# Moving shift rows from queries-on-partitions to rows: four TensorE transposes and a ScalarE copy, or one VectorE block transpose and four GpSimd copies

## What is computed

```
q, k, v = proj(xn, Wq, bq), proj(xn, Wk, bk), proj(xn, Wv, bv)      # (2, 16, 2048, 16)
idx = clip(r[None, :] - r[:, None], -128, 128) + 128
content = einsum('bhqd,bhkd->bhqk', q, k)
relative = einsum('bhqd,qkd->bhqk', q, rel_k[idx])
w = softmax((content + relative) / sqrt(16))
out = einsum('bhqk,bhkd->bhqd', w, v) + einsum('bhqk,qkd->bhqd', w, rel_v[idx])
s = out @ Wo.T + bo
h = gelu(einsum('td,edh->eth', xn, W1)); y = einsum('eth,ehd->etd', h, W2)
x + s * silu(y of the expert with the largest xn @ Wg + bg)
```

## Time and profile before

| | us |
|---|---|
| median of 3 runs | 2638.44 (2637.92 to 2640.88) |
| the profiled execution | 2641.73 |
| its span, first to last instruction | 2640.0 |
| PE busy | 2420.9 (92% of the span) |
| DVE busy | 1828.1 (69%) |
| ACT busy | 1749.4 (66%) |
| POOL busy | 884.5 (34%) |

### The profile page before, as it was taken

One profiled execution on the slowest core, in us unless ns is written; L12 is line 12 of the kernel. 1 busy time (PEld: TensorE's weight loads), 2 busy tenths in 40 slices (PEclk: granted clock), 3 DMA queues, 4 the chain that ended last, 5 costly groups with the idle time before them and its releaser, 6 DMA issues. The chain is left out here.

```text
span 2640.0 us, 47807 instructions
## 1 busy us (share of the span) xinstructions
PE 2420.9 (92%) x15216; PEld 1184.1 (45%) x15216; DVE 1828.1 (69%) x4985; ACT 1749.4 (66%) x4026; POOL 884.5 (34%) x1977
## 2 busy tenths in 40 slices
PE   6838999999999999999999999999999999799998
PEld 3412444444444444444444444444444444567666
DVE  6558777777777777777777777777777774233333
ACT  4514877777777777777777777777777777321121
POOL 1222454333333333333333333333333332133332
PEclk9955999999999999999999999999999999999999
DMA  5668889777777777777777777777777762642221
GB/s 160 176 141 265 244 268 243 235 222 230 233 230 237 225 222 233 234 231 236 232 228 234 231 236 236 231 226 226 233 231 238 227 194 88 244 144 69 66 64 53
DMA packets 351151, 541.00 MB, mean 205 GB/s; under 512 B 30608, under 2 KB 259392, under 8 KB 350912
## 3 DMA queue, kind: packets, MB, share of 16 engines
q1 hardware_dynamic: 336880, 502.76, 61.8%
q0 software_dynamic: 14032, 35.24, 4.5%
HBM read 272.60 MB, written 269.43 MB: 205 GB/s over the span
## 5 line engine op out<-in xcount | busy, mean ns | idle before, releaser
L1073 DVE TENSOR_REDUCE part<-ps 128x1 f32<-128x512 f32 (+3 forms) x2048 | 1189.5, 591 | 457.8 <-PE ps L957 438.8
L1135 ACT ACTIVATE probs_T<-pst 128x512 f32<-128x512 f32 (+3 forms) x2048 | 985.3, 525 | 397.4 <-PE pst L966 390.0
L957 PE MATMUL ps<-k_front,q_front 96*128 96x512 bf16 x2048 | 790.1, 393 | 13.0 <-DVE part L1071 2.5
L915 PE MATMUL pout<-probs_T,v_far 128*32 128x512 f32 (+3 forms) x4864 | 550.8, 533 | 40.4 <-ACT probs_T L1111 31.4
L822 POOL TENSOR_TENSOR left_T<-probs_T,left_mask 128x128 f32<-128x128 f32 x512 | 219.5, 429 | 991.7 <-ACT probs_T L1111 797.4
L957 PEld LDWEIGHTS ps<-k_front,q_front 96*128 96x128 bf16 x2048 | 198.6, 97 | 587.8 <-DVE part L1073 296.8
L966 PE MATMUL pst<-q_back,k_left 102*128 102x512 bf16 (+3 forms) x1024 | 349.7, 343 | 0.7 <-ACT probs_T L1135 0.6
L966 PE MATMUL pst<-q_back,k_right 102*128 102x512 bf16 (+3 forms) x1024 | 348.8, 342 | 0.5
L1148 ACT ACTIVATE band<-band,negm 128x384 f32<-128x384 f32 (+1 forms) x512 | 305.5, 597 | 0.1
L1071 DVE CUSTOM_DVE_ANT_0 band<-ps,band 128x256 f32<-128x256 f32 (+2 forms) x704 | 300.5, 427 | 0.0
L915 PEld LDWEIGHTS pout<-probs_T,v_far 128*32 128x32 f32 x4864 | 174.5, 108 | 237.9 <-issue 211.4
(11 more groups left out here) (160 smaller groups left out, 2112.0 us busy)
## 6 DMA issues: line engine op xcount, KB each, us to landing
rel_scores<-rel SPq DMA_DIRECT2D x128, 1024.0 KB, 7.9
band_probs<-band SPq DMA_DIRECT2D x128, 768.0 KB, 3.9
pwin<-band_probs SPq DMA_DIRECT2D x128, 512.0 KB
band<-rel_scores SPq DMA_DIRECT2D x64, 768.0 KB
band<-rel_scores SPq DMA_DIRECT2D x64, 576.0 KB, 5.2
w<-in_w_dram SPq DMA_DIRECT2D x16, 1024.0 KB, 14.3
band<-rel_scores SPq DMA_DIRECT2D x64, 128.0 KB, 5.7
q_terms<-terms SPq DMA_DIRECT2D x48, 128.0 KB
```

What stands on the lines that cost most here:

```text
L915: return nc.tensor.matmul(pout[32 * g:32 * g + 32, c0:c1], values, probs, start=first, stop=False, skip_group_check=True)
L957: nc.tensor.matmul(ps1[u % 2][:, :], q_front[a.par][:, a.s * P:(a.s + 1) * P], k_front[a.par][:, u * CW:(u + 1) * CW], start=True, stop=Tr ...
L1073: ins = nc.vector.tensor_reduce(peak, src, AX_X, ALU.max)
L1135: ins = nc.scalar.activation(probs_T[t.s % 2][:, u * CW + c0:u * CW + c1], pst[u % 2][:, c0:c1], ACT.Exp, scale=SCALE)
```

## The change

The shift values go into a `shb` of 32 columns for each block instead of 6 (zeroed once, so that the columns after the sixth are defined). In steps with off % 4 == 1, after the last maxima of the step, VectorE turns all 32x32 blocks of it into `shT` with one instruction of 128 partitions by 128 bf16. Query 32*b + c of block g then lies at partition 32*b + k, column (g, c), for shift row k. In steps with off % 4 == 2, at the very start of its step and so ahead of `left_T`, GpSimd copies the six rows of each of the four partition quarters into `q_back`, four instructions of 6 partitions by 4 x 32 bf16, each waiting for the one before. TensorE's four transposes, ScalarE's copy, and TensorE's waits that went with the shared bank are gone. Ahead of the copies GpSimd waits for VectorE's transpose, for earlier work of its own (`left_ready`, `sides_done`, `v_built`), and in hb 1 and 2 also for the `slot_tokens` DMAs of all steps before (`slots_filled`).

```diff
-        shb = two("shb", [P, CH, SHIFTS], BF16)
+        shb = two("shb", [P, CH, 32], BF16)
+        shT = sb("shT", [P, CH, 32], BF16)
-        prow = psmall[0:SHIFTS, NEARW:512].bitcast(BF16)
...
+                    pool.memset(shb[p][:, :, :], 0.0).then_inc(const_set, 1)
...
 # GpSimd, first thing in step(hb, off)
+                    q = Step(hb, off - 6)
+                    if off % CH == 2 and q.valid:
+                        pool.wait_ge(rows_tp, q.count(4, q.r + 1))
+                        if q.r == 0:
+                            wait(pool, st_mm, q.count(64, -64))
+
+                        left = Step(hb, off - LAG_T - 2)
+                        if left.valid:
+                            pool.wait_ge(left_ready, left.count(16, left.s + 1))
+                        sides = Step(hb, off + LAG_R - 4)
+                        pool.wait_ge(sides_done, sides.count(4, sides.r + 1) if sides.valid else NBH * 4)
+                        if off % NB == 10:
+                            pool.wait_ge(v_built, q.count(1, 1))
+                        if hb == 0:
+                            pool.wait_ge(slots_set, 16)
+                        if hb in (1, 2):
+                            pool.wait_ge(slots_filled, 16 * (TILES if hb == 2 else min(off, TILES)))
+                        rows = q_back[q.par][ROWS:ALLROWS, q.r * CW:(q.r + 1) * CW].rearrange("p (g b c) -> p b g c", g=CH, b=P // 32)
+                        for b in range(P // 32):
+                            if b > 0:
+                                pool.wait_ge(rows_link, q.count(12, 3 * q.r + b))
+                            ins = nc.gpsimd.tensor_copy(rows[:, b], shT[32 * b:32 * b + SHIFTS, :, :])
+                            ins.then_inc(rows_link if b < P // 32 - 1 else rows_copied, 1)
+                        pool.wait_ge(rows_copied, q.count(4, q.r + 1))
+
 # TensorE
-                    def shift_rows():
-
-                        pe.wait_ge(shift_ready, y.count(4, y.r + 1))
-                        wait(pe, rows_copied, y.count(4, y.r))
-                        if w.valid:
-                            wait(pe, winT_evac, w.count(16, w.s + 1))
-                        for g in range(CH):
-                            mm = nc.tensor.transpose(prow[0:SHIFTS, g * P:(g + 1) * P], shb[y.r % 2][:, g, :], con["ident_bf"][:, :])
-                        mm.then_inc(rows_tp, 1)
...
-                        if u == 1 and off % CH == 2 and y.valid:
-                            shift_rows()
...
-                        if off % CH == 2 and y.valid:
-                            pe.wait_ge(rows_copied, y.count(4, y.r + 1))
 # VectorE, after the maxima of u == 3
+                    def shift_rows():
+                        dve.wait_ge(shift_ready, shifted.count(4, shifted.r + 1))
+                        wait(dve, rows_copied, shifted.count(4, shifted.r))
+                        nc.vector.transpose(shT[:, :, :].rearrange("p g k -> p (g k)"), shb[shifted.r % 2][:, :, :].rearrange("p g k -> p (g k)")).then_inc(rows_tp, 1)
...
+                        if u == CH - 1 and off % CH == 1 and shifted.valid:
+                            shift_rows()
 # ScalarE
-                    def shift_rows():
-
-                        act.wait_ge(rows_tp, shifted.count(4, shifted.r + 1))
-                        nc.scalar.activation(q_back[shifted.par][ROWS:ALLROWS, shifted.r * CW:(shifted.r + 1) * CW], prow, ACT.Copy).then_inc(rows_copied, 1)
```

More of the change, by code:

```diff
@@ L605, in attend @@
         rows_tp = sem("rows_tp")
+        rows_link = sem("rows_link")
         rows_copied = sem("rows_copied")
@@ L683, in near_columns @@
             return bl[0] * P, (bl[-1] + 1) * P
-        CONSTS = 18
+        CONSTS = 20
         with nc.Block() as block:
@@ L828, in step @@
                         four = slice(4 * y.r, 4 * y.r + 4)
-                        t = shb[y.r % 2][:, :, :].rearrange("p g (k t) -> p g k t", k=2)
+                        t = shb[y.r % 2][:, :, 0:SHIFTS].rearrange("p g (k t) -> p g k t", k=2)
                         pool.wait_ge(rmax_ready, g + 1)
@@ L890, in step @@
                     w = Step(hb, off - LAG_T - 1)
-                    y = Step(hb, off - 6)
                     o = Step(hb, off - LAG_O)
                     ended = Step(hb, off - LAG_T - 2)
-                    def shift_rows():
-                        pe.wait_ge(shift_ready, y.count(4, y.r + 1))
-                        wait(pe, rows_copied, y.count(4, y.r))
-                        if w.valid:
-                            wait(pe, winT_evac, w.count(16, w.s + 1))
-                        for g in range(CH):
-                            mm = nc.tensor.transpose(prow[0:SHIFTS, g * P:(g + 1) * P], shb[y.r % 2][:, g, :], con["ident_bf"][:, :])
-                        mm.then_inc(rows_tp, 1)
                     def turn_back():
@@ L1023, in step @@
                     last = Step(hb, off - 1)
+                    shifted = Step(hb, off - 5)
                     four = slice(4 * last.r, 4 * last.r + 4)
@@ L1098, in step @@
                     y = Step(hb, off - 5)
-                    shifted = Step(hb, off - 6)
                     w = Step(hb, off - LAG_T - 1)
@@ L1140, in step @@
                             relative()
-                        if u == 1 and off % CH == 2 and shifted.valid:
-                            shift_rows()
                     if y.valid:
```

## The result

The change gains nothing: 2643.97 us (2639.76 to 2648.47, 10 runs) against 2638.49 (2633.72 to 2641.66, 10 runs), a ratio of 1.0021 with a 95% interval of 1.0011 to 1.0030. 2606 was predicted, with a range up to 2634. The span of the profiled execution is 2644.0 us against 2640.0.

The account below looks back on a forecast made before the run. PE's own work was taken to bound the kernel, with idle time before the transposes on its path. 2641.7 (profiled) - 66 (PE's gain) + 34 (second head's wait) = 2609.7, so a median of 2606 us; forecast 2592 to 2618, 8-in-10 range 2572 to 2634.

Parts of the forecast that it names:

- The bound and TensorE's gain: PE bounds the steps; without its transposes and their wait for VectorE's window it gains 65 to 67 us, taken as 66.
- ScalarE's copy, VectorE's transpose, GpSimd's copies: Removing 0.58 us copies gains nothing; a 0.25 us transpose and four 0.35 us copies a group cost nothing outside the second head.
- The room in steps 2 and 10: GpSimd's 1.75 us of copies a group fit without stopping PE: room 1.35 us in step 2, 1.1 in step 10.
- rival (c): Steps 2 and 10: GpSimd's copies across partition quarters are slow, from 0.6 us a copy; 2645 to 2720 us; chance 0.14.
- The added wait in the second head: Row copies wait for earlier slot_tokens DMAs, delaying left_T, ACT and PE: eight steps 3 to 5 us longer, 34 us lost.
- the landing time: In the second head a slot_tokens DMA takes 4.3 to 5.3 us from issue to landing, taken as 5.0.
- the slow copies of that end: Upper case for the second head's wait: slow GpSimd copies with a landing of 5.5 us, 45 us lost.

Follow-up runs that it names:

- the experiment with three copies: The changed kernel with slot_tokens DMAs issued two at a time (off % 4 of 2 and 3) and each GpSimd row copy done three times: 2703.88 us.
- the version with VectorE's copies: The changed kernel with the four row copies done by VectorE after its second reduction, without GpSimd's copies and their waits: 2603.18 us, ratio 0.9853.

## Why the prediction was wrong, point by point

**The bound and TensorE's gain: right.** A middle unit was to take 61.3 us and takes 61.11; steps 2, 6, 10, 14 were to take 5.8, 4.1, 3.6 and 3.5 to 3.65 and take 5.73, 4.09, 3.60 and 3.50. The gain in all is 71 us (75 lost, 4.0 of difference in the spans) where 66 was taken. PE has no wait for POOL left in the middle units.

**ScalarE's copy, VectorE's transpose, GpSimd's copies: right, with sizes a little off.** The transpose took 0.302 us and not 0.25, above the upper bound of 0.285, and it costs nothing that shows in a step. Here the Trainium skill had the better number (VectorE: DVE Perf Modes, The three transpose paths: 311 ns). A row copy takes 0.288 us:

```profile
L840 POOL COPY q_back<-shT 6x128 bf16<-6x128 bf16 x512 | 147.6, 288 | 108.3 <-DMA slot_tokens<-tok_i,pos_i 59.6 <-POOL rel L883 9.4 <-PE pst L983 6.9
```

**The room in steps 2 and 10, the place where rival (c) decides: right**, by the experiment with three copies. That rival did not come, since the copies across quarters cost no more than the fourth, which stays in its quarter (284 to 293 ns for all 512). (Its span in the prediction, 2645 to 2720, leaves out the lower end of its own working, 2637 at 0.73 us a copy.)

**The added wait in the second head: the failed step.** Its places and its chain were right, its price was 34 us and is 75. The term that was mis-sized is the landing time, "4.3 to 5.3 us from issue to landing", taken as 5.0. From the issue of the last DMA to the copies the changed kernel has 11.1 us (307.14 to 318.24) and 9.4 in the two steps 2, and 8.4 (336.75 to 345.14), 6.9, 8.0, 8.7, 7.3 and 8.0 in the other six places. Two things were wrong in reading it.

First, the DMA that was read in the earlier trace rows is the one of step 0. The one that the copies wait for is that of step 1, and it is issued together with the 1 MB write of `rel_scores`. Both were in the record of the kernel before: the write's row says 7.9 us to landing, and the packets of the DMA issued at 311.55, in step 1, went only from 317.4 on. The DMA ahead of that write, and so earlier, with the same wait behind it, brought back 57 us.

Second, packets are not landing. In the changed kernel the DMA queues have these rows, the first two for 336.7 to 342.7, the third for 342.7 to 345.2; the last two say what was issued in the first stretch, and the us to its landing:

```profile
q1 hardware_dynamic: 1591, 2.14, 103.6%
q0 software_dynamic: 64, 0.00, 0.7%
...
q1 hardware_dynamic: 336, 0.30, 46.0%
...
rel_scores<-rel SPq DMA_DIRECT2D x1, 1024.0 KB, 8.5
...
slot_tokens<-tok_i,pos_i POOLq DMA_INDIRECT x1, 8.2
```

All 64 packets of the software queue had gone by 342.7: 32 of the DMA issued at 333.12, by 338, and 32 of the one issued at 336.75, after 341.8. In the next 2.5 us only the hardware queue moved anything, and GpSimd still waited, to 345.14. So 5 of the 8.2 us passed before the DMA's packets went and more than 2 behind them, and it landed as the other queue's work drained: the write itself landed within 0.6 us of it in seven of the eight places. By packets alone the DMA of step 0 was probably read too short as well: in the changed kernel the one issued at 303.40 landed after 9.5 us.

The Trainium skill has a rule that bears on this (DMA: Bandwidth & Descriptors, Queues, rings and completion order): a completion increment is a strongly ordered write that lands only after every earlier write of that DMA engine, across its queues. These rows agree with it in part. The increment did come behind other traffic; but in five of the eight places the DMA landed ahead of the write, by 0.2 to 0.6 us in four and 1.7 in one, so it does not wait for the whole of a write that was issued before it. How much of the time behind the packets is this order and how much is plainly full engines, no run here separates.

PE's clock was not in the sum at all, so that a wait costs more than its length. PE is idle for 57.7 of the 75 us, and some 17 are its work at a lower granted clock, 0.70 to 0.81 in the eight long steps and 0.61 over the step 8 behind one of them.

With the eight landings as measured the prediction's own working gives 34 + 28 = 62 us for the wait, near the 57.7 that PE is idle, and 2641.7 - 66 + 62 = 2638 for a profiled execution that took 2645.6. The rest is the 17 us of the clock, less what the wait was taken too long by and the 5 us that the other units gained beyond 66.

The range failed with the term. Its upper end took the landing as 5.5 at most, from one DMA. With the measured mean of 8.5 and the slow copies of that end, the same working comes to 2641: nearer, and still short of 2644 without the clock.

## What to carry to other kernels

A wait for a small DMA costs what the traffic beside it costs: here it is priced far better by the landing of the largest transfer issued in the same moment than by its own packets, and not by another instance of the same DMA with other traffic beside it. When an engine gets a step that must wait for its own earlier DMAs, move the issues away from the wait in the same change; here that is the difference between 2644 and 2570 to 2575 us. And before four instructions are moved to another engine because they wait, see whether their order in the queue can be changed: that gave 47 of the 70 us.

## What the runs showed of the hardware that had not been expected

- GpSimd copies across partition quarters as fast as within one: 0.288 us for 6 partitions x 128 bf16, 284 to 293 ns over all 512, a fourth of which stay in their quarter; it is less than the 0.429 of a two-input 128x128 row.
- The same 6x128 copy takes 306 ns on ScalarE and 188 on VectorE. On ScalarE four of them (1.26 us) cost more than twice as much as the one of 6x512 from PSUM that they replaced (0.584).
- A small indirect DMA lands 2.2 to 10.9 us after its issue in one and the same kernel (6.0 at the median of 32, the changed kernel), by what the DMA engines have beside it.
- A VectorE copy from SBUF to SBUF waits while GpSimd issues an indirect DMA. In the version with VectorE's copies they take 188 ns at the median, in the second head up to 692, and four of them, started at 326.42 while GpSimd issued a DMA at 326.02 for 1.01 us, take 1.35 us in all; steps 6, 10 and 14 of that head are 0.2 to 0.5 us longer than in the others. The Trainium skill (SBUF — State Buffer, Who interferes with whom) says that VectorE in a two-port mode and GpSimd exclude each other. The trace agrees as far as the lengthened copies go; in which mode they ran it doesn't show.
